# Sliding-window attention in a fused AdaLN block: one row of 128 scores, and queries and keys of two tiles at once

## The chip, the cores and the metric

The kernel runs on one core of one Trainium2 chip. The metric is device time in microseconds (us), from the first instruction to the last. The core has five engines that run side by side and wait for each other through semaphores: TensorE (PE, with its weight loads as PEld), VectorE (DVE), ScalarE (ACT), GpSimd (POOL) and SyncE (SP), which here only issues transfers. PE writes into eight PSUM banks of 512 float32 columns, which DVE and ACT read; POOL reads SBUF alone.

## The reference, cut to what matters

The input is 4096 tokens of 256 values. An adaptive layer norm feeds sliding-window attention (4 heads of 64, window 128, with 64 memory rows ahead of the tokens); a two-layer MLP takes one gradient step towards the attention's output; its output is gated with the attention's, and a mixture of 64 experts follows. The change touches only the attention:

```
q, k, v = x_in @ wq.T, x_in @ wk.T, x_in @ wv.T          # x_in: 64 memory rows, then 4096 tokens
mask    = (j <= i) & (j > i - 128)
attn    = softmax(where(mask, q @ k.T / sqrt(64), -1e30))
swa     = (attn @ v) @ wo.T
```

## The kernel before

The program has three stages. Stage 1 (`memory_stage`) does the attention and the MLP's gradients; stage 2 (`token_stage`) gates, normalises and routes; stage 3 (`expert_stage`) runs the experts. The change is in stage 1.

Stage 1 walks over 33 tiles of 128 rows: tile 0 is the memory (64 rows of it empty), tiles 1 to 32 are the tokens. For every engine there is one function `body(n, q, pairs)`, whose order is written by hand: tiles 0 to 3 are unrolled, 28 tiles run in a hardware loop of four tiles per turn, and tile 32 is unrolled. `n` is the tile, `p` its parity. The four bodies meet at counting semaphores only.

In each body PE does in this order: queries and keys of tile n as float32 products (L966, eight products of 128 columns, each shown as two in the trace); the values (`values`); the turning of the error and of the attention's output of tile n-1 (`turn_error`); one k-half of the first hidden group; the scores (banks 3 and 4, 256 columns for each head: own tile and the tile before); the rest of the hidden layer; the weight gradients of a pair of tiles (`gradient`, 24 products of 512 columns); `backward` of tile n-1 (12 of 512); the turning of `prob` (eight blocks), of `h` (eight) and of the next tile's input (`turn_x`); attention times values ("o"); the prediction of the MLP (bank 7, 24 products of 256 columns); and the output projection ("swa").

Most products are split: each float32 operand is a high and a low part in a fast float32 format, and `mm_split` (L85) sums three products of them. So each operand needs a copy on ACT (high part) and a subtraction on DVE (low part) first.

Around the softmax, DVE adds the mask to each head's 256 scores and finds the maximum (L735, four times), negates the four maxima (L741), ACT takes the exponentials (L551, four of 256, after loading the table of Exp, L546), DVE takes reciprocals of the sums (L757) and POOL scales 1024 probabilities (L437). After PE has turned them, DVE copies one half out of PSUM (L778) and ACT the other (L571). ACT then needs the other table for the two sigmoids (L560, L561), after which it normalises the next tile (`normalise`, L487), DVE modulates it (`modulate`, L661 and L665), PE turns it (`turn_x`), and ACT and DVE make its two parts (`turned`, `turned_low`). One tile is prepared ahead.

Other lines that the steps touch: `pair_low` (L784) is the low part of the turned hidden values, which the prediction's products need; L826 is the low part of `h`; L815 and L712 make the error `e` of a tile from the prediction and `swa`; L804 scales `b2row` in tile 0; L586 and L416 are the high part of `h` (ACT) and the low part of `w2n` (POOL), both at the start; L627 are statistics of the input rows on DVE.

## Time and profile before

| | |
|---|---|
| median of 3 runs | 1868.12 us (1867.9 to 1870.27) |
| profiled execution: own time, span | 1868.3 us, 1866.6 us |
| PE busy over the span | 1818.9 us (97%) |
| DVE, ACT, POOL busy | 1231.6, 955.5, 950.5 us |
| stage 1, stage 2, stage 3 | 0 to 752, 752 to about 1230, then to 1866.6 us |

An engine's busy time counts its instructions from start to end. Successive matmuls overlap in the trace, so PE's rows are best read by the distance between starts. "Idle before" names what an engine waited for last.

### The profile page before, as it was taken

How to read it: one execution, taken by the hardware profiler on the slowest of the kernel's cores; microseconds unless marked ns; L12 is line 12 of the kernel's file. 1: busy time of each engine (PE TensorE's matmuls, PEld its weight loads, DVE VectorE, ACT ScalarE, POOL GpSimd, SP SyncE). 2: the span in 40 equal slices, each digit the busy share in tenths (PEclk: the TensorE clock that was granted, in tenths of full speed). 3: DMA queues.
4: the chain of work that ended last, by engine and by line, in shares of the span. 5: the costliest groups of instructions: out<-in, count | busy, mean ns of one | idle time of the engine just before them, and what ended most of it. 6: DMA issues, size and time to landing. Idle time of an engine off the chain costs nothing.

```text
span 1866.6 us, 36384 instructions
## 1 busy us (share of the span) xinstructions
PE 1818.9 (97%) x12428; PEld 1604.3 (86%) x12428; DVE 1231.6 (66%) x2454; ACT 955.5 (51%) x1789; POOL 950.5 (51%) x667
## 2 busy tenths in 40 slices
PE   7999999999999999999999999999999999999995
PEld 5788888888888888777888878889999999999994
DVE  8877777777777777567776668844555555555552
ACT  6666666666666665554453454334344444444341
POOL 5666566666656666026666656655333333323234
PEclk9999999999999999999999999999999999999998
DMA  6211111111111110302111011268898988888883
GB/s 230 68 38 39 34 34 37 34 34 37 37 34 34 53 34 21 120 27 74 46 47 46 1 45 43 89 208 265 266 289 293 292 288 265 289 291 285 279 288 81
DMA packets 141016, 234.08 MB, mean 125 GB/s; under 512 B 24756, under 2 KB 88971, under 8 KB 140816
## 3 DMA queue, kind: packets, MB, share of 16 engines
q1 hardware_dynamic: 116368, 220.50, 34.4%
q0 software_dynamic: 24576, 12.69, 4.5%
q8 instruction: 36, 0.59, 0.1%
q14 instruction: 36, 0.29, 0.1%
HBM read 194.58 MB, written 78.45 MB: 146 GB/s over the span
## 4 chain that ended last, share of the span: by engine, by line
PE 44%; DMA 9%; issue 3%; POOL 1%; DVE 1%; POOLq 0%; ACT 0%; SPq 0%; DVEq 0%; ACTq 0%
PE bank L85 24%; PE bank L1905 15%; DMA out_rows<-c_y_rest,c_token_rest 9%; PE bank L1169 4%; POOL out_rows L2079 1%; PE bank L1668 1%; PE bank L2127 1%; DMA c_w<-in_e1T 0%; DMA slots<-last_row,last_index 0%; POOL slots L1864 0%; POOLq L2088 0%; POOLq L67 0%; PE bank L2138 0%; DVE early L1547 0%; POOLq L2213 0%
## 5 line engine op out<-in xcount | busy, mean ns | idle before, releaser
L1905 PE MATMUL bank<-c_xT,c_w 128*128 128x160 f32 x3072 | 429.6, 299 | 3.0 <-DMA c_w<-in_e1T 2.4
L1905 PEld LDWEIGHTS bank<-c_xT,c_w 128*128 128x128 f32 x3072 | 419.2, 190 | 4.1 <-DMA c_w<-in_e1T 3.1
L1864 POOL DMA_INDIRECT slots<-b_row,b_index x224 | 249.9, 1116 | 193.8 <-issue 117.1
L2079 POOL DMA_INDIRECT out_rows<-c_y,c_x x64 | 100.7, 1574 | 372.0 <-DMA out_rows<-c_y_rest,c_token_rest 249.4
L2027 DVE TENSOR_TENSOR c_gT<-bank,c_sil 128x480 f32<-128x480 f32 x128 | 84.2, 658 | 210.8 <-PE bank L1905 210.8
L1995 ACT CAST c_gTs_high<-c_gT 128x384 fp32r<-128x384 f32 x128 | 65.6, 513 | 135.6 <-DVE c_gT L2027 135.6
L1988 ACT ACTIVATE c_sil<-bank 128x480 f32<-128x480 f32 x128 | 73.1, 571 | 109.8 <-PE bank L1905 109.3
L2020 DVE TENSOR_TENSOR c_gTs_low<-c_gT,c_gTs_high 128x384 fp32r<-128x384 f32 x128 | 71.7, 560 | 75.4 <-ACT c_gTs_high L1995 75.4
L456 POOL TENSOR_TENSOR last_row<-last_row,a_e 128x256 f32<-128x256 f32 x33 | 54.4, 1648 | 124.1 <-DVE a_e L712 122.4
L85 PE MATMUL bank<-c_w2s_high,c_gTs_high 128*128 128x256 f32 x384 | 114.0, 297 | 0.9 <-DVE c_gTs_low L2020 0.9
L85 PE MATMUL bank<-c_w2s_high,c_gTs_low 128*128 128x256 f32 x384 | 107.0, 279 | 0.0
L85 PE MATMUL bank<-c_w2s_low,c_gTs_high 128*128 128x256 f32 x384 | 106.9, 278 | 0.0
L437 POOL TENSOR_TENSOR a_prob<-a_prob,small 128x1024 f32<-128x1024 f32 x33 | 62.6, 1898 | 86.1 <-DVE small L757 86.1
L2079 POOL DMA_INDIRECT out_rows<-c_y_rest,c_token_rest x64 | 91.3, 1426 | 19.5 <-issue 19.5
L551 ACT ACTIVATE a_prob<-a_logit,small 128x256 f32<-128x256 f32 x132 | 65.6, 499 | 59.1 <-DVE small L741 59.1
L2002 ACT COPY c_xT<-bank 128x256 f32<-128x256 f32 x64 | 23.8, 372 | 124.6 <-PE bank L2127 87.6
L2020 DVE TENSOR_TENSOR c_w2s_low<-c_w,c_w2s_high 128x1536 fp32r<-128x1536 f32 x48 | 84.0, 1751 | 0.0
L444 POOL TENSOR_TENSOR last_row<-early 128x1024 f32<-128x1024 f32 x32 | 77.0, 2407 | 12.2 <-ACT early L560 12.2
L447 POOL TENSOR_TENSOR early<-last_row,early 128x1024 f32<-128x1024 f32 x33 | 78.2, 2370 | 7.6 <-DVE last_row L766 3.0
L1373 ACT ACTIVATE early<-bank,b1c 128x512 f32<-128x512 f32 x64 | 44.1, 691 | 73.5 <-PE bank L85 72.0
L425 POOL TENSOR_TENSOR a_dz_sum<-a_dz_sum,early 128x1024 f32<-128x1024 f32 x33 | 79.6, 2413 | 3.9 <-DVE a_dz_low L699 3.9
L451 POOL TENSOR_TENSOR a_gp<-early 128x1024 f32<-128x1024 f32 x33 | 80.0, 2426 | 2.6
(329 smaller groups left out, 5451.3 us busy)
## 6 DMA issues: line engine op xcount, KB each, us to landing
c_w<-in_e1T SPq DMA_DIRECT2D x64, 1536.0 KB, 7.0
c_w<-in_e2T SPq DMA_DIRECT2D x48, 768.0 KB, 9.1
early<-in_e2T SPq DMA_DIRECT2D x16, 768.0 KB, 8.8
slots<-a_fill SPq DMA_DIRECT2D x16, 642.0 KB, 3.9
c_x<-slots SPq DMA_DIRECT2D x64, 160.5 KB, 8.4
a_x_in<-in_x SPq DMA_DIRECT2D x32, 128.0 KB, 2.1
xT_tiles<-a_xT SPq DMA_DIRECT2D x32, 128.0 KB, 1.7
swaT_tiles<-a_swaT SPq DMA_DIRECT2D x32, 128.0 KB
```

The source lines that it names most:

```text
L85: ins = nc.tensor.matmul(out, a, b, start=first and i == 0, stop=last and i == 2, skip_group_check=True)
L425: pool.tensor_tensor(dz_sum[:], dz_sum[:], dz[:], ALU.add).then_inc(S("dz_sum"), 1)
L444: pool.tensor_tensor(h[:], zb[:], sg[:], ALU.mult).then_inc(S("h"), 1)
L447: pool.tensor_tensor(om[:], h[:], om[:], ALU.mult).then_inc(S("h_om"), 1)
L451: pool.tensor_tensor(gp[:], om[:], sg[:], ALU.add).then_inc(S("gp"), 1)
L1169: return nc.tensor.matmul(out, lhsT, rhs, start=first, stop=last, skip_group_check=True)
L1864: pool.indirect_dma_start(out=T["slots"], out_offset=bass.IndirectOffsetOnAxis(ap=index[:, t, k:k + 1], axis=0), in_=row[:, t, :], in_offs ...
L1905: return nc.tensor.matmul(out, lhsT, rhs, start=first, stop=last, skip_group_check=True)
L1988: act.activation(flat(sil[:, g * H:(g + 1) * H, :]), psum[1 + 2 * g][:, 0:H * CAP], ACT.Silu)\
L2020: return dve.tensor_tensor(out, raw, high.bitcast(F32), ALU.subtract)
L2027: dve.tensor_tensor(flat(gT[q][:, g * H:(g + 1) * H, :]), psum[2 + 2 * g][:, 0:H * CAP], flat(sil[:, g * H:(g + 1) * H, :]), ALU.mult).the ...
L2079: pool.indirect_dma_start(out=T["out"], out_offset=bass.IndirectOffsetOnAxis(ap=token, axis=0), in_=rows, in_offset=None, bounds_check=las ...
```

## The change

Query i of a tile sees exactly the keys j <= i of its own tile and j > i of the tile before. So both fit in one row of 128: ACT copies the previous tile's scores into `logit`, and DVE overwrites the places j <= i with the own tile's by a predicated copy. The queries are scaled by -1/8, so that a minimum over `logit` is the negated maximum. Exponentials, scaling and turning then work on 128 places a head. After turning, DVE multiplies by a triangle to get the own tile's part and subtracts it to get the other.

Queries and keys are made in odd tiles for two tiles at once, as 24 split products of 256 columns. For that the tiles are normalised, turned and split two ahead (`n + 2` where it was `n + 1`), and tile 0 prepares tiles 1 and 2. `kT` has three slots: POOL copies the even tile's keys to slot 0. PE turns `prob` before `backward`, and both k-halves of the first hidden group come before `turn_error`. Scaling by the row sums, the values, gradients and all else stay. The last four tiles of the loop are unrolled.

```diff
+Q_SCALE = -float(DH) ** -0.5
...
+        xm = [sb(f"xm{p}", [P, D]) for p in range(2)]
+        xms = [split(f"xms{q}", [P, D]) for q in range(4)]
         xT = sb("xT", [P, DC, P])
-        xTs = split("xT", [P, DC, P])
-        qT = split("qT", [P, DC, P])
-        kT = split("kT", [P, DC, 2, P])
+        xTs = split("xT", [P, DC, 2, P])
+        qT = split("qT", [P, DC, 2, P])
+        kT = split("kT", [P, DC, 3, P])
...
-        logit = sb("logit", [P, HEADS, 2 * P])
-        prob = sb("prob", [P, HEADS, 2 * P])
+        logit = sb("logit", [P, HEADS, P])
+        prob = logit
...
+        swaT = oT
...
+        def scores_of(b, slot):
+
+            return psum[3 + b][:, :].rearrange("p (c t j) -> p c t j", c=DC, t=2)[:, :, slot, :]
...
-            with eng.Fori(1, TILES // 4) as i:
+            with eng.Fori(1, TILES // 4 - 1) as i:
                 for q in range(4):
                     body(i * 4 + q, q, i * 2 + q // 2)
-            body(LAST, 0, LAST // 2)
+            for n in range(LAST - 4, LAST + 1):
+                body(n, n % 4, n // 2)
...
-                keep_xT(n)
+                if known(n, 1):
+                    keep_xT(n + 1)
                 keep_swaT(n - 1)
...
+                if q % 2 == 0 and n is not LAST:
+                    wait_apart(pool, S("qk"), pairs + 1, S("passed_pool"))
+                    if known(n, 1):
+                        wait_apart(pool, S("s_mm"), n, S("passed_pool"))
+                    for part in kT:
+                        ins = pool.tensor_copy(part[:, :, 0, :], part[:, :, 2, :].bitcast(F32))
+                    ins.then_inc(S("k_kept"), 1)
...
+                if not known(n, 1):
+                    pool.wait_ge(S("k_mm"), 1)
+                    weight_low(4, "wqk_low", wqk_raw, wqk)
                 pool.wait_ge(S("prec"), n + 1)
-                pool.tensor_tensor(prob[:], prob[:], prec.unsqueeze(2).to_broadcast([P, HEADS, 2 * P]),
+                pool.tensor_tensor(prob[:], prob[:], prec.unsqueeze(2).to_broadcast([P, HEADS, P]),
                                    ALU.mult).then_inc(S("prob"), 1)
...
-                wait_past(act, S("z_mm"), 2 * n)
-                act.copy(flat(xTs[0][:]), bank(6, D)).then_inc(S("xT_high"), 1)
+                wait_past(act, S("z_mm"), 2 * n - 2)
+                act.copy(xTs[0][:, :, 1 - p, :], bank(6, D).rearrange("p (c t) -> p c t", c=DC)).then_inc(S("xT_high"), 1)
...
             def normalise(n, p, loads):
 
+                act.wait_ge(S("xm"), n)
+                act.wait_ge(S("xT_low"), n)
...
+            def previous_scores(n):
+
...
+                act.wait_ge(S("s_mm"), n + 1)
+                first = P - MEM if not known(n, 2) else 0
+                for b in range(2):
+                    act.copy(logit[:, 2 * b:2 * b + 2, first:P], scores_of(b, 0)[:, :, first:P])\
+                       .then_inc(S("previous"), 1)
...
+                elif p:
+                    act.wait_ge(S("q_mm"), pairs + 1)
+                    act.wait_ge(S("s_mm"), n)
+                    act.activation(flat(qT[0][:]), bank(0), ACT.Copy, scale=Q_SCALE).then_inc(S("q_high"), 1)
+                    act.wait_ge(S("k_mm"), pairs + 2)
+                    act.wait_ge(S("k_kept"), pairs + 1)
+                    act.copy(kT[0][:, :, 1:3, :], bank(3).rearrange("p (c t j) -> p c t j", c=DC, t=2))\
+                       .then_inc(S("k_high"), 1)
...
+                    weight_high("wqk_in", flat(wqk_raw), flat(wqk[0][:]))
...
-                act.copy(xms[q][0][:], xm[:]).then_inc(S("xm_high"), 1)
+                act.copy(xms[q][0][:], xm[p][:]).then_inc(S("xm_high"), 1)
+                if known(n, 1):
+                    previous_scores(n)
...
-                wait_past(act, S("probT_mm"), 2 * n)
                 for s in range(HEADS):
-                    ins = act.activation(prob[:, s, :], logit[:, s, :], ACT.Exp, bias=npeak[:, s:s + 1],
+                    ins = act.activation(prob[:, s, :], logit[:, s, :], ACT.Exp, bias=npeak[:, s:s + 1], scale=-1.0,
...
+                elif ahead(n):
+                    normalise(n + 2, p, pairs + 1 + p)
...
-                act.wait_ge(S("probT_mm"), 2 * n + 2)
-                wait_past(act, S("o_mm"), n)
-                act.copy(flat(probT[:, 2:4, :, :]), bank(2)).then_inc(S("probT_hi"), 1)
...
+                if not known(n, 1):
+                    turned(1, 1)
+                    normalise(2, 0, 1)
+                elif ahead(n):
+                    turned(n + 2, p)
...
+                if not known(n, 1):
+                    turned(2, 0)
+                if known(n, 2) and not known(n, 3):
                     act.wait_ge(S("offset"), 2)
...
-            def modulate(n):
+            def modulate(n, p):
 
                 dve.wait_ge(S("xn"), n)
                 xn = psum[6][:, D:2 * D]
                 dve.tensor_tensor(xn, xn, mod[:, 1, :], ALU.mult).then_inc(S("xm_scaled"), 1)
...
+                wait_past(dve, S("xT_mm"), n - 1)
+                wait_past(dve, S("xm_low"), n - 1)
                 dve.wait_ge(S("xm_scaled"), n)
-                dve.tensor_tensor(xm[:], xn, mod[:, 0, :], ALU.add).then_inc(S("xm"), 1)
...
+            def part_prob(n, p):
+
+                dve.wait_ge(S("probT_mm"), n + 1)
+                wait_past(dve, S("o_mm"), n)
+                turned = bank(1).rearrange("p (s i) -> p s i", s=HEADS)
+                dve.tensor_tensor(probT[:, :, p, :], turned, own_T[:].unsqueeze(1).to_broadcast([P, HEADS, P]), ALU.mult)\
+                   .then_inc(S("probT"), 1)
+                dve.wait_ge(S("probT"), 2 * n + 1)
+                dve.tensor_tensor(probT[:, :, 1 - p, :], turned, probT[:, :, p, :], ALU.subtract).then_inc(S("probT"), 1)
...
+                elif p:
+                    dve.wait_ge(S("q_high"), pairs + 2)
+                    dve.scalar_tensor_tensor(out=flat(qT[1][:]), in0=bank(0), scalar=Q_SCALE,
+                                             in1=flat(qT[0][:]).bitcast(F32), op0=ALU.mult, op1=ALU.subtract)
+                    dve.wait_ge(S("k_high"), pairs + 2)
+                    dve.tensor_tensor(kT[1][:, :, 1:3, :], bank(3).rearrange("p (c t j) -> p c t j", c=DC, t=2),
+                                      kT[0][:, :, 1:3, :].bitcast(F32), ALU.subtract).then_inc(S("qk"), 1)
...
-                for s in range(HEADS):
-                    wait_past(dve, S("prob_exp"), n)
-                    wait_apart(dve, S("s_mm"), n + 1, S("passed_dve"))
-                    ins = dve.tensor_tensor_reduce(
-                        out=logit[:, s, :], in0=psum[3 + s // 2][:, (s % 2) * D:(s % 2 + 1) * D], in1=masks[:, mask, :],
-                        scale=float(DH) ** -0.5, scalar=-3e38, op0=ALU.add, op1=ALU.max, accum_out=peak[:, s:s + 1])
-                    if s % 2:
-                        ins.then_inc(S("peak"), 1)
-                dve.wait_ge(S("peak"), 2 * n + 2)
-                dve.tensor_scalar(npeak, peak, -1.0, None, ALU.mult).then_inc(S("npeak"), 1)
+                seen = slice(P - MEM if first else 0, P)
+                chosen = own[:, seen].unsqueeze(1).to_broadcast([P, DC, P - seen.start])
+                wait_apart(dve, S("s_mm"), n + 1, S("passed_dve"))
+                for b in range(2):
+                    if not first:
+                        wait_apart(dve, S("previous"), 2 * n - 1 + b, S("passed_dve"))
+                    dve.copy_predicated(logit[:, 2 * b:2 * b + 2, seen], chosen, scores_of(b, 1)[:, :, seen]).then_inc(S("picked"), 1)
+                dve.wait_ge(S("picked"), 2 * n + 2)
+                dve.tensor_reduce(npeak, logit[:], AX, ALU.min).then_inc(S("npeak"), 1)
...
+                elif ahead(n):
+                    modulate(n + 2, p)
+                if known(n, 2):
+                    part_prob(n, p)
                 if not first:
                     grad_z(n - 1)
-                dve.wait_ge(S("probT_mm"), 2 * n + 1)
-                wait_past(dve, S("o_mm"), n)
-                dve.tensor_copy(flat(probT[:, 0:2, :, :]), bank(1)).then_inc(S("probT_lo"), 1)
+                if not known(n, 2):
+                    part_prob(n, p)
...
                 if first:
-                    for c in (1, 2, 3):
+                    statistics(1)
+                    modulate(2, 0)
+                    for c in (2, 3):
...
-                elif known(n, 3) and not known(n, 4):
+                elif not known(n, 3):
                     deviations(1, range(1, CHUNKS))
...
+                if first:
+                    turned_low(2, 0)
...
-            def hidden_layer(n, g, ks):
+            def hidden_layer(n, p, g, ks):
+                if g == 1 and ks[0] == 0 and n is not LAST and known(n, 1):
+                    pe.wait_ge(S("xT_low"), n + 2)
...
+            def queries_and_keys(n):
+
+                pe.wait_ge(S("xT_low"), n + 2)
+                if not known(n, 2):
+                    pe.wait_ge(S("wqk_low"), 1)
+                wait_past(pe, S("dz"), 2 * n - 2)
+                for part, at, done in ((0, 0, "q_mm"), (1, 3, "k_mm")):
+                    for c in range(DC):
+                        for k in range(DC):
+                            ins = mm_split(nc, psum[at][:, c * D:(c + 1) * D],
+                                           cut(wqk, slice(None), part, k, slice(c * P, (c + 1) * P)),
+                                           [flat(a[:, k, :, :]) for a in xTs], k == 0, k == DC - 1)
+                    ins.then_inc(S(done), 1)
+
+            def turn_prob(n):
+
+                pe.wait_ge(S("prob"), n + 1)
+                if known(n, 2):
+                    pe.wait_ge(S("dW"), 4 * n - 7)
+                else:
+                    pe.wait_ge(S("v"), n + 1)
+                for head in range(HEADS):
+                    ins = turn(psum[1][:, head * P:(head + 1) * P], prob[:, head, :])
+                ins.then_inc(S("probT_mm"), 1)
...
-                pe.wait_ge(S("xT"), n + 1)
-                wait_past(pe, S("dz"), 2 * n - 2)
-                for j in range(4):
-                    for k in range(DC):
-                        ins = mm(psum[0][:, j * P:(j + 1) * P], wqk[:, j // 2, k, (j % 2) * P:(j % 2 + 1) * P],
-                                 xT[:, k, :], k == 0, k == DC - 1)
-                ins.then_inc(S("qk_mm"), 1)
...
+                elif p:
+                    queries_and_keys(n)
                 if not first:
-                    values(n)
+                    values(n, p)
                 if known(n, 1) and not known(n, 2):
                     modulations((2,))
                 if not first:
+                    hidden_layer(n, p, 0, (0, 1))
                     turn_error(n - 1)
...
-                pe.wait_ge(S("qk"), n + 1)
+                pe.wait_ge(S("qk"), pairs_done(q, pairs))
...
                 if known(n, 2):
                     gradient(n, q)
+                    turn_prob(n)
                 if not first:
                     backward(n - 1)
-
-                pe.wait_ge(S("prob"), n + 1)
-                for g in range(2):
-                    if known(n, 2):
-                        pe.wait_ge(S("dW"), 4 * n - 7 + g)
-                    else:
-                        pe.wait_ge(S("v"), n + 1)
-                    for b in range(4):
-                        ins = turn(psum[1 + g][:, b * P:(b + 1) * P],
-                                   prob[:, 2 * g + b // 2, (b % 2) * P:(b % 2 + 1) * P])
-                    ins.then_inc(S("probT_mm"), 1)
+                if not known(n, 2):
+                    turn_prob(n)
...
+                if first:
+                    turn_x(1, 1)
+                elif ahead(n):
+                    turn_x(n + 2, p)
...
-                pe.wait_ge(S("probT_lo"), n + 1)
-                pe.wait_ge(S("probT_hi"), n + 1)
+                pe.wait_ge(S("probT"), 2 * n + 2)
...
```

## Rows read from the trace of the kernel before

**Rows 1.** Busy time in a stretch: span, each engine's us, granted clock, DMA.

```profile
95.00:752.00 657.00, 655.87 (x4461) 570.55 (x4459) 499.63 (x1023) 416.18 (x890) 411.35 (x208) 1.00 0.11 36
```

**Rows 2.** Timeline of PE, one tile: start us, us, operation, idle before.

```profile
319.37 1.95 PE L256 MATMUL bank<-a_xT,a_wqk 128*128 128x128 f32 x16
321.07 0.37 PE L85 MATMUL bank<-a_wv_high,a_xT_high 128*128 128x256 f32 x1
...
323.99 0.50 PE L85 MATMUL bank<-w1T_high,a_xT_high 128*128 128x512 f32 x1
...
331.60 0.39 PE L85 MATMUL bank<-a_w2n_high,a_eT_high 128*128 128x512 f32 x1
...
334.33 1.04 PE L870 MATMUL bank<-ident,a_prob 128*128 128x128 f32 x8
335.20 1.04 PE L870 MATMUL bank<-ident,last_row 128*128 128x128 f32 x8
...
336.39 1.09 PE L256 MATMUL bank<-a_probT,a_v 128*64 128x128 f32 x16
337.41 0.39 PE L85 MATMUL bank<-w2T_high,pair_high 128*128 128x256 f32 x1
...
340.25 1.02 PE L256 MATMUL bank<-a_woT,a_oT 128*128 128x256 f32 x4
341.12 1.95 PE L256 MATMUL bank<-a_xT,a_wqk 128*128 128x128 f32 x16
```

**Rows 3.** Timeline of DVE in the same tile.

```profile
324.25 0.42 DVE L735 CUSTOM_DVE_ANT_0 a_logit<-bank,a_masks 128x256 f32<-128x256 f32 x1 [0.42 <-PE bank L256]
...
325.76 1.12 DVE L741 TENSOR_SCALAR small<-small 128x4 f32<-128x4 f32 x1
...
331.89 0.69 DVE L708 TENSOR_TENSOR a_dW<-a_dW,bank 128x512 f32<-128x512 f32 x1 [0.67 <-PE bank L85]
332.80 0.43 DVE L661 TENSOR_TENSOR bank<-bank,mod 128x256 f32<-128x256 f32 x1 [0.23 <-ACT bank L487]
...
333.71 1.51 DVE L692 TENSOR_TENSOR early<-bank,a_gp 128x512 f32<-128x512 f32 x2
...
336.51 1.29 DVE L784 TENSOR_TENSOR pair_low<-bank,pair_high 128x512 fp32r<-128x512 f32 x2 [0.69 <-ACT pair_high L575]
```

**Rows 4.** Timeline of ACT in the same tile.

```profile
322.89 0.39 ACT L499 COPY a_swaT<-bank 128x256 f32<-128x256 f32 x1
...
323.60 1.28 ACT L546 ACT_TABLE_LOAD   x1
...
326.91 0.51 ACT L551 ACTIVATE a_prob<-a_logit,small 128x256 f32<-128x256 f32 x1 [1.81 <-DVE small L741]
...
332.22 0.55 ACT L487 ACTIVATE bank<-a_x_in,a_offset,small 128x256 f32<-128x256 f32 x1
```

**Rows 5.** Timeline of all engines, end of tile 0 and start of tile 1.

```profile
29.39 1.05 ACT L586 CAST a_h_high<-last_row 128x1024 fp32r<-128x1024 f32 x1 [3.92 <-DVE w2T_low L622]
...
32.32 4.57 POOL L416 TENSOR_TENSOR a_w2n_low<-a_dW,a_w2n_high 128x2048 fp32r<-128x2048 f32 x1 [4.10 <-ACT a_w2n_high L472]
...
32.92 1.37 DVE L627 BATCH_NORM_STATS2 a_stats<-a_raw 128x6 f32<-128x256 f32 x4
...
34.79 1.88 PE L256 MATMUL bank<-a_raw,a_swaT 128*128 128x512 f32 x4
...
36.33 0.70 DVE L804 TENSOR_SCALAR a_b2row<-a_b2row,a_step 128x256 f32<-128x256 f32 x1
...
38.38 1.15 DVE L826 TENSOR_TENSOR a_h_low<-last_row,a_h_high 128x1024 fp32r<-128x1024 f32 x1
...
41.16 0.50 PE L85 MATMUL bank<-w1T_high,a_xT_high 128*128 128x512 f32 x1
```

**Rows 6.** Timeline of PE where stage 2 begins; eleven matmuls are left out.

```profile
754.06 0.76 PE L85 MATMUL bank<-pair_high,w1T_high 128*128 128x512 f32 x1 [2.25 <-PEq L103]
...
759.15 0.40 PE L85 MATMUL bank<-pair_high,w1T_high 128*128 128x512 f32 x1
```

More of the change, by code:

```diff
@@ L193, in memory_stage @@
         rstd = small[:, 0:TILES]
-        peak, npeak, psums, prec = (small[:, TILES + a * HEADS:TILES + (a + 1) * HEADS] for a in range(4))
+        npeak, psums, prec = (small[:, TILES + a * HEADS:TILES + (a + 1) * HEADS] for a in range(3))
         odd = 4 * UNIT + 2 * UNIT + 81 * UNIT + UNIT + 2 * P + UNIT
@@ L598, in body @@
                 act.copy(swa[:], psum[7][:, D:2 * D]).then_inc(S("swa"), 1)
-                if known(n, 3) and not known(n, 4):
+                if not known(n, 1):
+                    turned(2, 0)
+                if known(n, 2) and not known(n, 3):
                     act.wait_ge(S("offset"), 2)
-            turned(0)
+            turned(0, 0)
             tiles(act, body)
@@ L827, in body @@
                    .then_inc(S("h_low"), 1)
-            turned_low(0)
+                if first:
+                    turned_low(2, 0)
+            turned_low(0, 0)
             statistics(0)
@@ L938, in gradient, with values @@
                     else:
-                        pe.wait_ge(S("peak"), 2 * n + j - 1)
-            def values(n):
-                wait_past(pe, S("probT_lo"), n)
+                        pe.wait_ge(S("picked"), 2 * n + j - 1)
+            def values(n, p):
+                wait_past(pe, S("probT"), 2 * n)
                 pe.wait_ge(S("xT_low"), n + 1)
@@ L1051, in body @@
                 ins.then_inc(S("swa_mm"), 1)
-            turn_x(0)
+                if first:
+                    turn_x(2, 0)
+            turn_x(0, 0)
             tiles(pe, body)
```

174 lines of the change are left out of this document (94 added, 80 removed).

## The prediction

> **What bounds the kernel now.** I read the page first (each engine's busy share, and the slices, where PE stands at nine tenths nearly everywhere), then the busy time of each engine in the stretch of stage 1, then the timelines of one tile in the loop, engine by engine, and last those of the start. In stage 1 PE is busy 655.87 of 657 us, DVE 499.63 [rows 1]. From tile to tile PE's list repeats after 21.75 us (319.37 to 341.12) with no idle time [rows 2]. So a tile takes what PE's list takes, as long as the others deliver in time; the reader is to see in [rows 3, 4] how near they are. Two marks serve below: S, the end of the scores (323.99), and G, the end of the weight gradients (331.60) [rows 2].
>
> **PE's list.** Removed in each tile: the float32 products for queries and keys, 1.70 us (319.37 to 321.07), and four of eight turned blocks of `prob`, half of 0.87 us (334.33 to 335.20), 0.44 [rows 2]. Added in odd tiles: 24 split products of 256 columns. The prediction's 24 of the same shape take 2.84 us (337.41 to 340.25) with a change of shape of 0.1 in it, so 2.75; in the odd tile that change is the one that the removed products had. Changes of shape elsewhere: turned error to hidden layer and hidden layer to scores go, `prob` to `backward` comes; taken at nothing, with 0.1 us a tile either way as bound. Even tile: 21.75 - 1.70 - 0.44 = 19.61. Odd tile: 19.61 + 2.75 = 22.36. A pair: 41.97 for 43.50.
>
> **Does the next tile begin in time?** An even tile has no queries and keys ahead of `turn_error`, only the values and the two k-halves, 2.2 us. The error is made by ACT's copy of `swa` and two passes of DVE, and is complete 1.6 us after the projection's end in today's timeline; it hides with 0.5 to spare. S then lies at 2.92 (321.07 to 323.99) + 0.68 for the second k-half = 3.6 us into the tile. In odd tiles 2.75 us lie before all that. There ACT and DVE make four parts of 512 values at some 0.6 us each; DVE is free at 2.7 (after L826), so `qk` is complete at 4.3, and the scores are due at 5.3. POOL's two copies of keys (0.4 each for 256 values) fall into its idle time, behind `e_sum`.
>
> **From scores to the next stage of the tile.** S to G shrinks from 7.61 to 6.93, since one k-half (0.68) moved ahead of S; so the chain beside PE has 0.68 less time. It is:
> ACT: two copies of 256 previous scores, at most 0.39 each as L499, done at S + 0.95; the table load that stood at S - 0.4 (323.60) now follows them, 1.28 and 0.2, to S + 2.4 [rows 4].
> DVE: two predicated copies of 256. The trace has none. L735 does two sources for 256 values in 0.42 [rows 3]; one that also reads its old output would at worst be a second pass, 0.84. I take 0.42, the row that it is nearest to, and keep 0.84. Then the minimum over 512 values, priced as DVE's other passes over 512, 0.69 (331.89). Done at S + 2.3.
> The exponentials began at S + 2.92 (326.91) and begin at S + 2.4. Four of 128 values save 0.11 each (0.51 for 256 now; bounds nothing and half). So `normalise` starts at S + 7.25 for S + 8.23 (332.22) and ends, 0.55 later, at G + 0.9 for G + 1.17 [rows 4].
> DVE: the last gradient gather starts at G + 0.29 (331.89), so L661 starts at G + 0.95; modulation 0.91 (332.80 to 333.71); the two products for `probT`, the second waiting for the first, 0.83 + 0.65, where L778 cost 0.6 later; L692 twice, 1.3. `pair_low` starts at G + 4.65, its first half done at 5.34 [rows 3].
> PE: turning 0.44 + 0.1, `backward` 2.73, so `h` is turned from G + 3.27; 1.19 to the attention product, 1.02 to the prediction, G + 5.48 [rows 2]. That leaves `pair_low` 0.1 us. Before, it started when ACT's high part was there, with DVE idle 0.69 [rows 3]: this cover is used up. I add 1 us in all for it (0.03 a tile); each 0.1 us more is 3 us.
> POOL's `prob` is half as long and ends near S + 5.2; its turning is due at S + 6.93. L571 leaves ACT. None of that sets the end.
>
> **L741.** It negates four numbers and takes 1.12 us, since POOL's sum of 2.4 us runs beside it (min 0.17, in tile 0) [rows 3]. L627, with one input, ran 1.37 us for four beside POOL's L416 as it does alone [rows 5]. The minimum replaces L741, and I take it as L627: not held.
> The Trainium skill, page "SBUF — State Buffer", section Who interferes with whom, says that on this chip a scalar operation of VectorE can take the port pair shared with GpSimd and is then shut out whole, and a reduction never; by that rule the sum stays, and without it the first rival below would be the forecast.
>
> **The start.** Tile 1 now needs tile 2 split as well. ACT's `normalise(2)` waits for the low part of tile 1, made just before the first chunk of statistics, at 31.3 (one chunk of 1.72 before 32.92). It stands ahead of L586, which moves from 29.39 to 32.0; so L416 on POOL, behind it, ends 2.65 later than 36.89, at 39.55 [rows 5]. L804, a scalar operation, was held until 36.9 (0.70 long); on DVE it would come at 37.5 (modulation 0.91 and a second product 0.67 more, 0.4 less by a shorter `prob`), and is held to 39.6. From it to the end of L826 it is 2.5 us (37.03 to 39.53), then 0.4 for the low part of tile 2: 42.55 [rows 5]. PE waits for this before its first product of tile 1; before, only `e` and the low keys came late, and queries, values and modulation lay ahead of them. From there: 2.75, values 0.7, modulation 1.88, k-halves 1.45, error 0.4, scores 0.9: 8.1 us. After an idle time of 8 us the clock: after 2.25 us of it twelve distances took 5.09 us (754.06 to 759.15) where `backward`'s twelve take 2.73, which is 1.2 for 2.4 GHz; so 2.4 more [rows 2, 6]. S of tile 1 is at 53.1 for 41.16: +11.9. In tile 1 the two `probT` products stand behind L692, and the attention product starts 1.0 us later after S. Sum +12.9. If DVE's work in tile 0 moves less, 10; if the idle time also cools stage work behind it, 16.
>
> **Sum.** Even tiles 4 to 32: 15 x -2.14 = -32.1. Odd tiles 5 to 31: 14 x 0.61 = +8.5. Tile 2: -1.6 (two chunks of statistics of 1.72 stand before the reciprocals and cost 1.35 of waiting for `prob`, but a wait for `h` goes). Tile 3: +0.9, as 13 small operations for the deviations come before its error. Tile 4: -0.7, which they cost there now. Start +12.9. `pair_low` +1.0. In all -11.1. The profiled execution took 1868.3 us (span 1866.6), the median is 1868.12: 1868.3 - 11.1 = 1857. Stages 2 and 3 only start earlier; the last tile's code is straight-line already and repeats after the same 21.75 us, so unrolling costs nothing.
>
> **Rivals.**
> 1. The minimum is held by POOL as L741 is (slower). POOL's sum starts after the later `xm_low`, S + 1.0, and ends at S + 3.4; the minimum, begun after that, ends 1.7 us later. With 0.3 of slack, 1.4 us x 31 = +43: 1900. It decides as soon as the hold is over 0.7 us (11.1 / 31 + 0.3). For: L741, L804. Against: L627. Chance 0.06.
> 2. DVE becomes the bound: predicated copies at 0.84. Both lie on the chain, 0.84 more; minus 0.3 of slack, 0.5 us x 31 = 17: 1874. At 0.62 each it comes out at 1861, at 0.75 it eats the gain. Chance of 1864 to 1872: 0.13; of more: 0.05.
> 3. The change of lead costs little: DVE's second tile is hidden, start at +5 and no late `pair_low`: 1848 to 1850. For: DVE has gaps in tile 0. Against: L804 and the wait on tile 2's low part at the end of the body. Chance 0.10.
> 4. The change does not do what it says: split products at 256 columns no faster than float32. Against: 2.75 for two tiles and 3.40 stand in [rows 2]. No chance of its own.
> Forecast, 1850 to 1864: 0.66.
>
> Below 0.2%, 3.7 us, a measurement of this kernel can't tell a difference. Faster 0.66 + 0.10 = 0.76; same 0.13; slower 0.11. The range, 1848 to 1868, takes in the third rival and half the second.
>
> **What would show it.** In the loop: distances of the projections alternating 19.6 and 22.4; no idle time of PE before the prediction's first product; L741's successor under 0.8 us; `normalise` ending 0.9 after G; in tile 1 PE idle about 8 us from 34.5, and its matmuls at half clock behind. The prediction is wrong if the minimum or the predicated copies last over 0.7 us, if `turn_error` waits in even tiles, or if the start loses another 5 us.

## The result, and the profile after

The changed kernel takes 1859.45 us (median of five; 1859.06 to 1860.99), the kernel before 1869.42 beside it: a ratio of 0.995, interval 0.9935 to 0.9964, so 0.5% faster. The profiled execution took 1860.99 (span 1859.3) where the one before took 1868.3: 7.3 less, for a forecast of 11.1 less.

The page of the changed kernel, its busy times and its clock:

```profile
PE 1802.1 (97%) x12168; PEld 1583.7 (85%) x12168; DVE 1220.6 (66%) x2257; ACT 946.0 (51%) x1789; POOL 942.5 (51%) x695
PEclk8999999999999999999999999999999999999998
```

PE is still the engine that binds, at 97%; the granted clock is at 0.9 or more everywhere but in the first and the last slice (0.8). So there are two questions: what the loop does, and what the start does.

**The loop.** The timeline of PE over an odd tile and the even one behind it (the first row of each group of products; compare [rows 2]; L270 and L86 are the helpers that L256 and L85 were, L957 turns blocks):

```profile
303.48 1.03 PE L270 MATMUL bank<-a_woT,a_oT 128*128 128x256 f32 x4
304.15 0.47 PE L86 MATMUL bank<-a_xT_high,a_wqk_high 128*128 128x256 f32 x1
...
307.07 0.28 PE L86 MATMUL bank<-a_wv_high,a_xT_high 128*128 128x256 f32 x1
...
325.93 1.03 PE L270 MATMUL bank<-a_woT,a_oT 128*128 128x256 f32 x4
326.60 0.47 PE L86 MATMUL bank<-a_wv_high,a_xT_high 128*128 128x256 f32 x1
...
327.48 0.39 PE L86 MATMUL bank<-w1T_high,a_xT_high 128*128 128x512 f32 x1
...
330.30 0.50 PE L86 MATMUL bank<-w1T_high,a_xT_high 128*128 128x512 f32 x1
...
337.30 0.60 PE L957 MATMUL bank<-ident,a_logit 128*128 128x128 f32 x4
337.65 0.48 PE L86 MATMUL bank<-a_w2n_high,a_eT_high 128*128 128x512 f32 x1
...
340.52 1.03 PE L957 MATMUL bank<-ident,last_row 128*128 128x128 f32 x8
...
342.73 0.39 PE L86 MATMUL bank<-w2T_high,pair_high 128*128 128x256 f32 x1
...
345.66 1.03 PE L270 MATMUL bank<-a_woT,a_oT 128*128 128x256 f32 x4
```

From projection to projection the odd tile takes 22.45 us (303.48 to 325.93), the even one 19.73 (325.93 to 345.66), and no row has idle time. The forecast was 22.36 and 19.61. All pairs of the loop repeat this within 0.01; the unrolled tiles 31 and 32 take 22.21 and 19.58.

The other engines in the even tile, first DVE, then POOL, then ACT:

```profile
330.99 0.78 DVE L816 COPY_PREDICATED a_logit<-a_own,bank 128x256 f32<-128x256 int32 x2 [0.24 <-ACT a_logit L532]
331.81 0.69 DVE L818 TENSOR_REDUCE small<-a_logit 128x4 f32<-128x512 f32 x1
...
338.19 0.43 DVE L719 TENSOR_TENSOR bank<-bank,mod 128x256 f32<-128x256 f32 x1
...
341.77 1.29 DVE L864 TENSOR_TENSOR pair_low<-bank,pair_high 128x512 fp32r<-128x512 f32 x2
```

```profile
331.69 2.42 POOL L443 TENSOR_TENSOR a_dz_sum<-a_dz_sum,early 128x1024 f32<-128x1024 f32 x1
```

```profile
332.54 0.39 ACT L605 ACTIVATE a_logit<-a_logit,small 128x128 f32<-128x128 f32 x1
...
337.41 0.55 ACT L521 ACTIVATE bank<-a_x_in,a_offset,small 128x256 f32<-128x256 f32 x1
```

With S (the end of the scores) at 330.30 and G (the end of the gradients) at 337.30, one sees: both predicated copies in 0.78 us (mean of one 0.443, where 0.42 was taken); the minimum in 0.69 although POOL's dz_sum covers all of it (331.69 to 334.11), where L741 took 1.12 in the same place [rows 3]; the exponentials from S + 2.24; `normalise` done at G + 0.66; `pair_low` from G + 4.47 with its first half done 0.3 before the prediction's first product. DVE has 0.2 of slack ahead of L719 as well (ACT was done at 337.96). So the chain has some 0.5 us to spare.

**The start.** One timeline over all engines, from tile 0 into tile 1 (compare [rows 5]):

```profile
15.00 2.38 POOL L433 TENSOR_TENSOR a_wqk_low<-a_wqk,a_wqk_high 128x1024 fp32r<-128x1024 f32 x1
15.12 2.80 DVE L679 TENSOR_TENSOR a_wv_low<-last_row,a_wv_high 128x512 fp32r<-128x512 f32 x1
...
35.67 4.50 POOL L433 TENSOR_TENSOR a_w2n_low<-a_dW,a_w2n_high 128x2048 fp32r<-128x2048 f32 x1 [6.56 <-ACT a_w2n_high L503]
...
38.34 1.98 DVE L889 TENSOR_SCALAR a_b2row<-a_b2row,a_step 128x256 f32<-128x256 f32 x1
...
42.75 0.40 DVE L728 TENSOR_TENSOR a_xT_low<-bank,a_xT_high 128x256 fp32r<-128x256 f32 x1
...
43.20 0.58 PE L86 MATMUL bank<-a_xT_high,a_wqk_high 128*128 128x256 f32 x1 [7.93 <-DVE a_xT_low L728]
...
53.98 0.50 PE L86 MATMUL bank<-w1T_high,a_xT_high 128*128 128x512 f32 x1 [0.96 <-DVE mod L703]
...
61.87 1.10 PE L957 MATMUL bank<-ident,last_row 128*128 128x128 f32 x8 [2.81 <-POOL last_row L475]
...
64.38 1.98 PE L270 MATMUL bank<-a_probT,a_v 128*64 128x128 f32 x16 [1.20 <-DVE a_probT L782]
```

PE waits 7.93 us for the low part of tile 2. And the windows of two stretches of tile 1 (span, busy us of PE, PEld, DVE, ACT, POOL, granted clock, DMA share, GB/s):

```profile
43.00:46.50 3.50, 3.30 (x15) 3.30 (x16) 0.15 (x1) 0.33 (x1) 0.65 (x2) 0.50 0.00 0
64.40:70.50 6.10, 6.10 (x35) 5.77 (x36) 4.77 (x14) 3.67 (x4) 2.37 (x1) 0.50 0.01 3
```

The granted clock is 0.50, that is 1.2 GHz, twice: behind the wait of 7.93, and again behind waits of 2.81 and 1.20 in tile 1. Tile 1's projection starts at 71.14; before it was at 55.71. Tile 32's starts at 724.89 for 731.69.

Behind stage 1 nothing was altered in any kernel here, yet from the projection of tile 32 to the end of the span it took between 1133.7 and 1136.7 us over the thirteen profiles. That is why the table below gives the starts of the projections of tiles 1 and 32 beside the medians: a few us are read better there.

### The profile page after: what moved, and what is told of

Read it like the earlier page. It is cut to its first block, busy times and chain, and to the rows that moved or that the text cites. A ratio compares the mean times of both kernels' runs of the same rounds, so it can differ in the third digit from the quotient of the medians.

```text
span 1859.3 us, 35688 instructions
## 1 busy us (share of the span) xinstructions
PE 1802.1 (97%) x12168; PEld 1583.7 (85%) x12168; DVE 1220.6 (66%) x2257; ACT 946.0 (51%) x1789; POOL 942.5 (51%) x695
## 4 chain that ended last, share of the span: by engine, by line
PE 54%; DMA 2%; DVE 1%; issue 1%; POOL 1%; ACT 0%; POOLq 0%; SPq 0%; DVEq 0%; ACTq 0%
PE bank L86 26%; PE bank L2013 23%; PE bank L1277 4%; DMA out_rows<-c_y_rest,c_token_rest 2%; PE bank L2235 1%; POOL out_rows L2187 1%; PE bank L1776 1%; DMA c_w<-in_e1T 0%; DMA slots<-last_row,last_index 0%; PE bank L2246 0%; POOL slots L1972 0%; DVE c_y_rest L2154 0%; DVE early L1655 0%; POOLq L2321 0%; PE bank L2240 0%
## 5 line engine op out<-in xcount | busy, mean ns | idle before, releaser
L86 PE MATMUL bank<-c_w2s_high,c_gTs_high 128*128 128x256 f32 x384 | 114.0, 297 | 0.9 <-DVE c_gTs_low L2128 0.9
L86 PE MATMUL bank<-c_w2s_high,c_gTs_low 128*128 128x256 f32 x384 | 106.9, 279 | 0.0
L86 PE MATMUL bank<-c_w2s_low,c_gTs_high 128*128 128x256 f32 x384 | 106.9, 278 | 0.0
L627 ACT CAST pair_high<-bank 128x512 fp32r<-128x512 f32 x66 | 35.5, 589 | 102.8 <-PE bank L957 102.8
L86 PE MATMUL bank<-w2T_high,pair_high 128*128 128x256 f32 x264 | 78.6, 298 | 1.9 <-DVE pair_low L864 1.7
```

The lines of the kernel that those rows point to most:

```text
L86: ins = nc.tensor.matmul(out, a, b, start=first and i == 0, stop=last and i == 2, skip_group_check=True)
```

## The experiments

| kernel | tile 1 | tile 32 | median | ratio to before, interval |
|---|---|---|---|---|
| before | 55.71 | 731.69 | 1869.42 to 1870.92 | 1 |
| changed | 71.14 | 724.89 | 1859.45 | 0.995, 0.9935 to 0.9964 |
| the same once more | 70.70 | 724.46 | 1860.86 | 0.9946, 0.993 to 0.9961 |
| PE's order in tile 1 | 68.38 | 722.22 | 1859.61 | 0.9939, 0.9922 to 0.9955 |
| order of tile 0 | 63.49 | 717.21 | 1856.31 | 0.9922, 0.9906 to 0.9939 |
| both orders | 61.55 | 715.48 | 1851.84 | 0.9895, 0.9878 to 0.9911 |
| three orders | 59.07 | 712.83 | 1848.92 | 0.9883, 0.9857 to 0.9909 |
| scores alone | 58.61 | 721.05 | 1857.98 | 0.9924, 0.9907 to 0.994 |
| scores alone, start mended | 57.44 | 719.88 | 1856.58 | 0.9914, 0.989 to 0.9939 |
| scaling of b2row early | 70.14 | 724.04 | 1859.37 | 0.9932, 0.9908 to 0.9956 |
| scalar operation put back | 70.88 | 753.77 | 1889.92 | 1.01, 1.0069 to 1.0132 |
| two minima | 70.82 | 727.03 | 1865.42 | 0.9972, 0.9955 to 0.9988 |
| prob turned late | 69.72 | 763.28 | 1900.88 | 1.0154, 1.0113 to 1.0196 |

The second row of the changed kernel was made for comparison, with this expectation: 

> The changed kernel once more, with nothing altered, so that the runs beside it have it on the same chip. Any theory: 0.995 of the kernel before, 19.73 and 22.45 us in the loop.

### What the score part is worth without the pairing

This kernel is the one before, with only the score part of the change; queries and keys stay as they were:

```diff
-                act.copy(flat(qT[0][:]), bank(0, D))
+                act.activation(flat(qT[0][:]), bank(0, D), ACT.Copy, scale=Q_SCALE)
...
+                    dve.copy_predicated(logit[:, 2 * b:2 * b + 2, seen], chosen, scores_of(b, p)[:, :, seen]).then_inc(S("picked"), 1)
+                dve.wait_ge(S("picked"), 2 * n + 2)
+                dve.tensor_reduce(npeak, logit[:], AX, ALU.min).then_inc(S("npeak"), 1)
...
                     gradient(n, q)
+                    turn_prob(n)
                 if not first:
                     backward(n - 1)
```

> Kernel before with the score part of the change alone: one row of 128 scores, predicated copies, minimum, the triangle for the turned probabilities, both k-halves ahead of the error's turning, prob turned before backward. Queries and keys stay float32 products of one tile, and tiles are prepared one ahead. Theory (the pairing of queries and keys gains 0.65 us a pair in PE's list, 10 us over stage 1, and costs all of the start's 15.4): 21.43 us a tile for 21.75 (the 19.73 of an even tile plus 1.70), so -0.32 x 31 = -10, start as in the kernel before: about 1858, no slower than the full change. Rival (the shorter chain only pays with the pairing, since tile by tile the copies, minimum and triangle are late): over 21.6 us a tile and 1864 or more.

Two projections that follow each other on PE:

```profile
337.22 1.02 PE L263 MATMUL bank<-a_woT,a_oT 128*128 128x256 f32 x4
...
358.55 1.02 PE L263 MATMUL bank<-a_woT,a_oT 128*128 128x256 f32 x4
```

Every tile of the loop takes 21.33 us, 0.42 less than before and 0.10 less than expected, even and odd. Tile 32 is reached at 721.05, 3.4 to 3.8 us ahead of the full change. The full change beats it in the loop, 42.18 for 42.66 a pair, 0.48 where 0.65 had been expected, and from tile 1 to tile 32 it is 8.7 us faster (653.75 for 662.44); but it reaches the end of tile 1 12.1 to 12.5 us later (70.70 and 71.14 for 58.61). So as it was made, the pairing loses more at the start than it gains behind it, and the score part alone gives the whole gain.

The start of this kernel is not that of the kernel before, as had been expected: its tile 1 ends 2.9 us later (58.61 for 55.71). PE waits 2.81 us there for `h` and 1.00 for `probT`, and the granted clock behind that is 0.50; in the kernel before, after waits of 1.22, 1.53 and 0.47 us in the same tile, it stays at 1.00. The windows of PE (span, busy us, granted clock, DMA share, GB/s), first of this kernel, then of the kernel before:

```profile
54.00:56.00 2.00, 2.00 (x12) 0.50 0.00 0
```

```profile
50.00:52.00 2.00, 1.48 (x14) 1.00 0.00 0
```

The 3 us gained in the loop beyond the expectation (31 times 0.10) and these 2.9 nearly cancel, so the time came out at the 1858 that was expected partly by luck.

### What the start costs, and whose it is

First PE's order in tile 1 alone:

```diff
+                second = known(n, 1) and not known(n, 2)
+                if second:
+                    values(n, p)
+                    hidden_layer(n, p, 0, (0, 1))
-                elif p:
+                if p:
                     queries_and_keys(n)
```

> Changed kernel; in tile 1 only, PE makes the values and the first hidden group (both k-halves) before the queries and keys, so 2.15 us of its work stand in the idle time of 7.93 us that lies ahead of them. Theory (the start is set by the low part of tile 2, which ends at 43.15, and PE's list behind it counts in full): the first product of the queries and keys stays at 43.2, tile 1's end moves from 71.14 to about 68.8, the span shrinks by 2 to 3 us, more if the half clock behind goes too. Rival (the queries' and keys' two parts on ACT and DVE set the scores, not PE's list): the scores come at most 0.5 us earlier and the span stays within 1 us.

Tile 1 ends 2.3 to 2.8 us earlier, tile 32 2.2 to 2.7: PE's list behind the wait counts in full. In the total it can hardly be told.

Then tile 0's order on ACT and DVE:

```diff
                 act.copy(hsp[p][0][:], h[:]).then_inc(S("h_high"), 1)
                 if not known(n, 1):
                     weight_high("w2n_in", flat(dW2[:]), flat(w2n[0][:]))
+                    normalise(2, 0, 1)
...
                     dve.tensor_scalar(step[:], theta[:], -1.0, None, ALU.mult).then_inc(S("rates"), 1)
+                    dve.tensor_scalar(b2row[:], b2row[:], step[:, 0:1], None, ALU.mult).then_inc(S("b2row"), 1)
...
                     statistics(1)
                     modulate(2, 0)
-                    for c in (2, 3):
-                        statistics(c)
+                    statistics(2)
+                    turned_low(2, 0)
+                    statistics(3)
```

> Changed kernel; tile 0's order on ACT and DVE only: the high parts of h and w2n stand ahead of the normalising of tile 2, b2row is scaled as soon as the step is known (31.4), the low part of tile 2 stands ahead of the error and of the last chunk of statistics. Theory (ACT's and DVE's order in tile 0 makes the idle time of 7.93 us, half of it by the hold that POOL's w2n_low puts on the scaling of b2row): the first product of the queries and keys moves from 43.20 to 37 to 38, tile 1's scores end at 45 to 46 for 53.98, the half clock in tile 1 goes, span shorter by 9 to 12 us, to about 1848. Rival (turning, normalising and splitting tile 2 is late by its own chain, whatever the order): first product not before 41, span shorter by under 3 us. In both the loop keeps its 19.73 and 22.45 us.

```profile
37.03 0.39 PE L86 MATMUL bank<-a_xT_high,a_wqk_high 128*128 128x256 f32 x1 [1.59 <-DVE a_xT_low L728]
...
47.73 0.50 PE L86 MATMUL bank<-w1T_high,a_xT_high 128*128 128x512 f32 x1 [0.95 <-DVE mod L703]
```

The first product of the queries and keys comes at 37.03 for 43.20, after 1.59 us of idle time for 7.93. Tile 32 comes 7.3 to 7.7 us earlier, less than the 9 to 12 expected; the half clock in tile 1, which was to go, stayed (the projection at 63.49). It stayed in both places: the queries and keys run at half clock though PE's waits ahead of them are now only 1.74 and 1.59 us, with two turned blocks between. With both edits:

> The two edits of the start together. Theory: PE's idle time ahead of the queries and keys of tile 1 falls to about 1 us, tile 1 ends near 57.5, close to the 55.7 of the kernel before, and the span is 12 to 15 us shorter than the changed kernel's, 1844 to 1847. Rival: with the low part of tile 2 early, PE's order no longer matters and the time is that of the run with the start's order alone.

Tile 32 is reached at 715.48, 1.7 ahead of the order of tile 0 alone, where 2.15 us of PE's work had been moved; the rival, no gain, is out. The first stretch of half clock is gone: PE goes straight from a wait of 1.75 us into the values, the hidden layer and the queries and keys. One window of PE there, with the order of tile 0 alone and with both:

```profile
39.00:41.00 2.00, 2.00 (x11) 0.52 0.00 0
```

```profile
39.00:41.00 2.00, 2.00 (x14) 1.00 0.00 0
```

The scores of tile 1 come 3.4 us sooner by it, but tile 1 ends at 61.55 where 57.5 had been expected, and the kernel takes 1851.84 us for an expected 1844 to 1847. What is left is tile 1's second half. There PE waits 1.21 us for the products of `probT`, which stand behind the modulation and the gradient on DVE, though DVE was idle before:

```diff
+                if known(n, 1) and not known(n, 2):
+                    part_prob(n, p)
                 if first:
                     modulate(1, 1)
```

> The two edits of the start, and in tile 1 DVE makes the two products for probT ahead of the modulation of tile 3 and of the error's gradient (in the run before, PE waited 1.21 us for them there, and ran at half clock for some 6 us after it). Theory (idle time ahead of the attention product lets the clock fall): the wait of 1.21 goes, and with it the half clock, worth 2.9: tile 1 ends at 57 to 58 for 61.55, tile 32 at 711 to 712 for 715.5, time 1847 to 1849. Rival (the clock falls from the longer wait of 2.81 us for h ahead of it): only 1.2 us are gained, tile 1 ends at 60.3.

Windows of PE (span, busy us, granted clock, DMA share, GB/s), with both orders:

```profile
54.00:56.00 2.00, 1.29 (x12) 0.57 0.04 8
56.00:58.00 2.00, 2.00 (x14) 0.50 0.00 0
58.00:60.00 2.00, 2.00 (x12) 0.50 0.00 0
```

and with three:

```profile
54.00:56.00 2.00, 2.00 (x17) 0.50 0.03 8
56.00:58.00 2.00, 2.00 (x17) 0.88 0.00 0
58.00:60.00 2.00, 2.00 (x16) 1.00 0.00 0
```

The wait of 1.21 is gone, the wait of 2.82 for `h` ahead of it is not, and the clock still falls, but for some 3 us instead of 6. Tile 1 ends 2.5 us earlier (59.07), between the two expectations: the shorter idle time brought the clock back sooner, it did not keep it. With three orders the kernel takes 1848.92 us, 1.2% less than the kernel before, and some 11 us less than the change as it was made. The fair comparison is then the score part alone with the same edit in tile 1:

> Kernel with the score part alone, with the products for probT first in tile 1 on DVE. It is the fair opponent of the run with three orders: both have the start mended. Theory (the pairing of queries and keys is worth 0.65 less 0.18 us a pair, that is 42.18 for 42.66, 7.4 us in 15.5 pairs, less 2 us for what is left of its start): this kernel at 1853 to 1855, 4 to 6 us behind the three orders; against the score part alone it gains 1 to 4 us. Rival (the mended pairing is worth nothing in the sum): both within 2 us.

It takes 1856.58 us, tile 32 at 719.88: 7 us behind the three orders in stage 1, and 7.7 in the medians, where 4 to 6 had been expected. Its own gain of 1.2 us in stage 1 is at the lower end of what was expected, and in the medians (1857.98 and 1856.58) it can't be told. So the pairing pays, once its start is mended. One edit of the three orders could have helped this kernel too and was not tried in it, the early scaling of `b2row`; PE's waits ahead of the scores of its tile 1, which are all that it could shorten, are 0.42 and 1.08 us, so most of the 7 us stays with the pairing.

### What was held by POOL

First only the scaling of `b2row` is moved, to where the step's rate is known:

> Changed kernel with only the scaling of b2row moved, to right behind the step's rate (31.4), ahead of POOL's w2n_low. In the changed kernel it took 1.98 us for 0.29 to 0.40, until 40.3. Theory A (the two scalar operations that make the error, behind it, are not held, since they read PSUM or run alone): the low part of tile 2 ends 1.5 to 2 us sooner, at about 41.4, and the span shrinks by as much. Theory B (those are held by the same w2n_low, until 40.17): the hold only passes to the next operation, the low part of tile 2 ends at 42.9 to 43.1, nothing changes beyond 0.4 us.

DVE at the end of tile 0, and POOL's `w2n_low` there:

```profile
38.73 0.45 DVE L900 SCALAR_TENSOR_TENSOR a_e<-bank,a_step,a_b2row 128x256 f32<-128x256 f32 x1
39.22 1.62 DVE L771 SCALAR_TENSOR_TENSOR a_e<-a_swa,a_theta,a_e 128x256 f32<-128x256 f32 x1
```

```profile
36.06 4.50 POOL L433 TENSOR_TENSOR a_w2n_low<-a_dW,a_w2n_high 128x2048 fp32r<-128x2048 f32 x1 [7.03 <-ACT a_w2n_high L503]
```

Half of either theory. The first operation of the error, which reads one operand from PSUM, took 0.45 in the middle of POOL's subtraction. The second, which reads both from SBUF, took 1.62 and ended at 40.84, 0.28 after POOL. So the hold passed on, and tile 2's low part began at 42.23 for 42.75 (tile 0's projection at 32.37 and 32.36 in the two runs). The Trainium skill, page "SBUF — State Buffer", section Who interferes with whom, states that a DVE instruction with two SBUF inputs contends with a GpSimd instruction that reads SBUF, and that one with at most one SBUF input, outside the two-port modes, does not; these two rows agree.

Then the same question where rival 1 put it, behind the minimum in each tile:

```diff
-                dve.tensor_reduce(npeak, logit[:], AX, ALU.min).then_inc(S("npeak"), 1)
+                dve.tensor_reduce(peak, logit[:], AX, ALU.min).then_inc(S("peak"), 1)
+                dve.wait_ge(S("peak"), n + 1)
+                dve.tensor_scalar(npeak, peak, 1.0, None, ALU.mult).then_inc(S("npeak"), 1)
```

> Changed kernel with the scalar operation over four numbers put back behind the minimum (times 1.0, 0.17 us when nothing holds it). Theory (a scalar operation on DVE beside POOL's dz_sum is held until that ends, a reduction is not): it lasts to the end of the dz_sum, some 1.2 us after the minimum; the exponentials begin 1.2 us later, and with the 0.5 us of slack that the trace of the changed kernel shows (0.2 ahead of the modulation, 0.3 between the first half of pair_low and the prediction) a tile is 0.6 to 0.8 us longer: +19 to +25 us, about 1882. Rival (the hold in the kernel before came from something else, or the chain has over 1.2 us of slack): the operation takes 0.2 us and the time stays within 2 us. If there is no slack at all: +1.2 a tile, +38 us.

DVE in an even tile, POOL beside it, and PE ahead of the prediction one tile earlier:

```profile
345.13 0.69 DVE L818 TENSOR_REDUCE small<-a_logit 128x4 f32<-128x512 f32 x1
345.86 1.58 DVE L820 TENSOR_SCALAR small<-small 128x4 f32<-128x4 f32 x1
```

```profile
345.00 2.41 POOL L443 TENSOR_TENSOR a_dz_sum<-a_dz_sum,early 128x1024 f32<-128x1024 f32 x1
```

```profile
336.44 0.36 PE L86 MATMUL bank<-w2T_high,pair_high 128*128 128x256 f32 x1 [0.61 <-DVE pair_low L866]
```

The minimum takes 0.69 inside POOL's sum, the scalar operation behind it 1.58, to 347.44, when POOL ends (347.41). `pair_low` now makes PE wait 0.61. Even tiles take 20.8 us (+1.1), odd ones 23.2 (+0.8); tile 32 comes 29 us later, and the median is 29 us higher, more than the 19 to 25 expected: slower than the kernel before. The delay of the exponentials is 1.6 us in the even tile and 1.25 in the odd, so 0.45 to 0.55 of it was slack.

### How much slack the chain has

```diff
+                wait_past(dve, S("peak"), n)
+                dve.tensor_reduce(peak, logit[:], AX, ALU.min).then_inc(S("peak"), 1)
                 dve.tensor_reduce(npeak, logit[:], AX, ALU.min).then_inc(S("npeak"), 1)
```

> Changed kernel with the minimum made twice, the first into four unused numbers: 0.6 us more of DVE between the scores and the exponentials, the same as predicated copies at twice their price would have been. Theory (0.5 us of slack in the chain): 0.1 to 0.2 us a tile, +3 to +6 us. Rival A (the chain is tight, as the prediction took it with 0.1 to 0.3): 0.4 to 0.5 us a tile, +12 to +16 us. Rival B (DVE's chain is far from binding): no change.

About half of the tiles of the loop stay at 19.73 and 22.45, the others take 0.1 to 0.2 more; tile 32 comes 2.1 to 2.6 us later, under 0.1 us a tile. The median is 4.6 us above that of the changed kernel beside it, of which stage 1 explains half. The slack of 0.5 us is confirmed from the other side. Rival 2 reckoned with 0.3 of slack; by that, 0.6 us more of DVE would have cost 0.3 us a tile.

The last run puts the turning of `prob` back behind `backward`:

```diff
                     gradient(n, q)
-                    turn_prob(n)
                 if not first:
                     backward(n - 1)
-                if not known(n, 2):
-                    turn_prob(n)
+                turn_prob(n)
```

> Changed kernel with prob turned after backward, as before the change. It saves a change of shape on PE (0.1 us a tile). Theory (the cover of the two products of probT is backward's 2.73 us): they are then late for the attention product, which starts some 0.5 to 1.5 us later in each tile: +15 to +45 us. Rival (DVE has them in time behind h's and x's turning, 1.2 us): the loop shrinks by 0.1 us a tile, -3 us.

DVE and PE with `prob` turned behind `backward`:

```profile
332.74 0.69 DVE L779 TENSOR_TENSOR a_probT<-bank,a_own_T 128x512 f32<-128x512 f32 x1 [1.56 <-PE bank L957]
```

```profile
334.21 1.09 PE L270 MATMUL bank<-a_probT,a_v 128*64 128x128 f32 x16 [0.41 <-DVE a_probT L782]
...
336.09 0.35 PE L86 MATMUL bank<-w2T_high,pair_high 128*128 128x256 f32 x1 [0.79 <-DVE pair_low L864]
```

DVE stands idle 1.56 us for the turned probabilities, and then everything behind them is late: PE waits 0.41 for `probT` and 0.79 for `pair_low`, 1.2 us a tile; tile 32 comes 38 to 39 us later, and the median is 40 us higher. The place of the turning, ahead of `backward`, is what lets the two products replace one copy at no cost.

## Why the prediction was right, and where it was off

The direction, the mechanism and the place of gain and loss were right; two terms were too small, PE's list by 3 us over the loop and the start by 2.5, and one was too large, 1.0 for `pair_low`. By the projections that makes 6.8 us of gain for 11.1; that the time still came within 2.5 us of the forecast (1859.45 for 1857) is in part luck, as the last points show. By its steps (the tiles as distances of projections, against before):

- **PE's list.** Right. Even 19.73 for 19.61, odd 22.45 for 22.36, both inside the bound of 0.1 for the changes of shape but for 0.02. A look at the even tile says where: `backward` takes 2.87 (337.65 to 340.52) for 2.73 behind its new change of shape and the prediction 2.93 for 2.84, and the projection gives way to the values 0.2 sooner (after 0.67, 325.93 to 326.60, for 0.87). The rest is spread over the tile: the turning of the error 0.16 more, the values 0.10, the gradients 0.05, the hidden layer 0.14 less, `prob` 0.09 less than forecast. Why the unchanged prediction takes 0.09 more stays open. 0.12 and 0.09 a tile make 3 us over the loop.
- **The chain from the scores.** Right, with too little slack: 0.1 was left for `pair_low`, 0.3 was there, and 0.2 more ahead of the modulation. The 1.0 us added for it did not come.
- **L741.** Right: the minimum is not held (0.69 us), and the run with the scalar operation put back shows what was at stake. Rival 1 priced it at +43 us for a hold of 1.7; the hold that the run made is 1.2 to 1.6 and costs 29, with slack of 0.5 for the 0.3 assumed.
- **Rival 2.** It did not come: the predicated copies take 0.443 each. Two minima put 0.6 us more on the same chain and cost under 0.1 us a tile; copies at twice their price would put on nearly 0.9, which with 0.5 of slack makes some 0.4 us a tile, an estimate from these runs, near the 0.5 that the rival gave for 0.84. What ruled it out is the price of the copies, which no row of before had.
- **The start.** This is the term that was mis-sized: 15.4 us (55.71 to 71.14; 15.0 in the same kernel once more) for 12.9.
- **The start up to the scores.** Up to the scores of tile 1 it came out, by two errors that cancel. The low part of tile 2 ends at 43.15 for 42.55. Most of this 0.6 is the input's arrival in this run: DVE's first statistics wait for it until 7.79 us, until 7.23 in the same kernel once more (7.14 before), and there the low part ends at 42.63. The kernel's own share, made good on the way to the low part, is 0.4 at the end of tile 0 (projection at 31.84 for 31.45), and it had no term: POOL's new `wqk_low`, 2.38 us from 15.00, runs beside DVE's subtraction for `wv_low`, which takes 2.80 where the same shape took 0.68 before. The score part alone, without `wqk_low`, has 0.68 there too and the projection at 31.47. Then, from PE's first product to the end of the scores, it took 9.75 us for the forecast's 10.5, as the half clock cost 1.6 us (fifteen products in 3.37) and not 2.4 (the modulation, taken at a row's 1.88, is 1.32 from start to start, and the k-halves, turning and products of the keys make up for it); so the scores ended at 52.95 (the last wait for `mod` of 0.96 is behind them) for 53.1.
- **The start behind the scores.** Here 1.0 was allowed for, and 3.6 came: 0.96 for `mod`, which hid behind the k-half that had been moved ahead of the scores, and 2.9 for the second stretch at half clock, 64.4 to 70.5 (the attention product to the projection in 6.76 us for 3.88), with 0.3 gained elsewhere. The prediction named it ("if the idle time also cools stage work behind it, 16") and did not take it. And this stretch is not the pairing's: the score part alone has it too, and its tile 1 ends 2.9 us later than before.
- **Tiles 2 to 4.** -1.8, +1.0 and -2.7 for -1.6, +0.9 and -2.8. Right.
- **The sum.** From the tiles measured, tile 32 is 6.8 us earlier. The profiled executions are 7.3 apart. That the medians lie 10 us apart, near the forecast of 11.1, is not explained by any of its terms: the kernel before had 1868.12 in the three runs that the forecast started from, and then 1869.42 to 1870.92. Where the other 3 us lie is not shown.
- **Rival 3, a cheap start,** did not come in the change, but it is what the three orders made: 1848.92, inside the 1848 to 1850 that it was given, by another way (the order of tile 0, not a hidden DVE).

## What to carry to other kernels

A change that gains some tenths in each turn of a loop has to be charged for its first turn: here the pairing of two tiles gained 8.7 us behind tile 1 and lost 12 by making tile 1 wait for tile 2, and three edits that only put existing operations of the first two tiles in another order were worth some 11 us, about as much as the whole change. Read what stands on each engine's queue ahead of the one operand that the new lead needs, and put behind it all that is not due yet; and where an idle stretch can't be removed, keep it short, as the clock behind it costs again (1.6 and 2.9 us here). Prefer to feed a waiting engine from an operation that GpSimd's work beside it does not hold: here a reduction of 0.69 us ahead of the exponentials for a scalar operation of up to 1.6.

## What the runs showed of the hardware

- A reduction over 512 values on VectorE took 0.69 us in the middle of a GpSimd addition of 2.4 us; a scalar operation over four values behind it took 0.85 to 1.60 us in the loop, and ended with the addition (347.44 and 347.41).
- A two-operand VectorE operation was held by GpSimd to the end of its subtraction with both operands in SBUF (1.62 us for 0.48), and not with one in PSUM (0.45).
- A predicated copy of 256 values from PSUM, with its mask in SBUF, took 0.443 us (mean of 58), as much as a plain operation of the shape (0.41 to 0.43), with GpSimd's subtraction or addition beside part of it.
- TensorE's granted clock was 0.50 (1.2 GHz) behind idle times of 7.93 us, and of 2.81 and 1.21 (or 1.00) with little work between them; with only the 2.82 left it fell too, for half as long. Behind 1.74 and 1.59 us with two turned blocks between, it was 0.52; behind 1.75 us followed by work without a pause, 1.00. In the kernel before, waits of 1.22, 1.53 and 0.47 us in tile 1 did not bring it down.
